# Attention's values made once per token and copied to their windows, 4 KB runs in the last stage, and column factors in PSUM in the sampling stage

## What is computed

```python
x = x + deformable_conv(group_norm(x))     # 8 groups, 9 points each, bilinear sampling, mask
t = tokens(x)
t = t + local_attention_block(layer_norm(t))   # 8 heads of 32, values of 16
t = t + moe_ffn(layer_norm(t))             # 8 experts, the best 2 for each token, 128 -> 512 -> 128
# inside the attention block: each token looks at itself and 32 tokens on either side
scores[w] = q[s] . k[s + w - 32] / sqrt(32) + rel_bias[w]     # w = 0..64, NEG outside the image
out = softmax(scores) @ v[s - 32 .. s + 32]
# moe: out[token] = weight[0] * expert_a(token) + weight[1] * expert_b(token)
```

## Time and profile before

| | us |
|---|---|
| three timed runs | 1660.62, 1667.56, 1667.63 (median 1667.56) |
| profiled execution, own time | 1650.45 |
| its span, first to last instruction | 1648.6 |
| PE busy | 1273.7 (77%) |
| DVE busy | 1039.2 (63%) |
| ACT busy | 762.2 (46%) |
| POOL busy | 631.1 (38%) |
| mean granted TensorE clock | 0.89 of full speed |

### The profile page before, as it was taken

How to read it: one execution, slowest core, us unless ns; L and a number is a source line. 1 busy time by engine, 2 the same in 40 slices (tenths; PEclk the granted TensorE clock), 3 DMA queues, 4 the chain that set the end, 5 groups by cost and what they waited for, 6 DMA issues and landing times. The chain is left out here.

```text
span 1648.6 us, 42938 instructions
## 1 busy us (share of the span) xinstructions
PE 1273.7 (77%) x13859; PEld 827.0 (50%) x13860; DVE 1039.2 (63%) x2372; ACT 762.2 (46%) x2018; POOL 631.1 (38%) x678
## 2 busy tenths in 40 slices
PE   4962898888989875898787888577752389999974
PEld 1541343433434322666565666233322389999972
DVE  4995889889898422676576677256553434444435
ACT  1212443444434260655454555375551157777650
POOL 2000788877878600000000000005677445555550
PEclk9995899999999995999899999797765589999995
DMA  3000000000000000000000000401111122222219
GB/s 112 0 0 11 0 1 1 0 0 0 0 0 0 5 0 25 3 4 4 4 4 4 3 4 4 164 1 37 43 48 50 47 54 66 68 68 68 66 53 304
DMA packets 56950, 54.72 MB, mean 33 GB/s; under 512 B 10335, under 2 KB 48735, under 8 KB 56439
## 3 DMA queue, kind: packets, MB, share of 16 engines
q1 hardware_dynamic: 46071, 31.12, 6.7%
q0 software_dynamic: 8448, 17.58, 3.2%
q10 hardware_dynamic: 2304, 4.20, 0.7%
HBM read 29.93 MB, written 23.00 MB: 32 GB/s over the span
## 5 line engine op out<-in xcount | busy, mean ns | idle before, releaser
L2073 ACT ACTIVATE e_hT<-e_ph,e_b 128x128 f32<-128x128 f32 x544 | 155.4, 369 | 74.7 <-PE e_ph L2030 58.1
L433 POOL TENSOR_TENSOR s_pc<-s_wide,VP 128x512 f32<-128x512 f32 x112 | 157.1, 1403 | 53.8 <-ACT s_wide L506 47.1
L1326 ACT ACTIVATE a_E<-a_E,a_nm 128x96 f32<-128x96 f32 x512 | 142.7, 361 | 68.7 <-DVE a_nm L1402 68.4
L424 POOL TENSOR_TENSOR s_acc<-s_acc,s_pb 128x512 f32<-128x512 f32 x112 | 153.9, 1374 | 40.6 <-DVE s_pb L585 39.0
L656 PE MATMUL s_pbc<-s_AT,s_sel 120*128 120x512 bf16 x400 | 135.3, 388 | 40.0 <-DVE s_pa L585 26.9
L1596 POOL MEMSET m_total<- 128x8 f32 x1 | 0.1, 110 | 410.7 <-POOLq L1138 410.7
L667 PE MATMUL s_pout<-s_pa,s_opT 128*128 128x512 f32 x288 | 151.6, 607 | 0.0
L2041 PE MATMUL e_py<-e_w,e_hT 128*128 x1088 | 149.3, 280 | 1.8 <-ACT e_hT L2073 1.2
L2030 PE MATMUL e_ph<-e_xT,e_w1s 128*128 128x128 f32 x1088 | 147.2, 279 | 1.0 <-issue 0.7
L1612 POOL DMA_INDIRECT slots<-m_pay,m_pos x128 | 127.7, 998 | 42.2 <-issue 42.2
L2011 POOL DMA_INDIRECT picks<-e_yw,e_rows x136 | 134.7, 991 | 22.5 <-POOL e_tick L2009 20.6
(11 more groups left out here) (218 smaller groups left out, 2518.1 us busy)
## 6 DMA issues: line engine op xcount, KB each, us to landing
e_rows<-slots SPq DMA_DIRECT2D x136, 66.0 KB
c_y<-picks SPq DMA_DIRECT2D x32, 256.0 KB
X<-in_x SPq DMA_DIRECT2D x8, 512.0 KB, 8.3
e_w<-in_w SPq DMA_DIRECT2D x2, 2048.0 KB, 12.7
out<-c_o ACTq DMA_DIRECT2D x16, 256.0 KB
picks<-e_yw,e_rows POOLq DMA_INDIRECT x136
slots<-m_pay,m_pos POOLq DMA_INDIRECT x128
m_pad<-in_c_pad SPq DMA_DIRECT2D x1, 1056.0 KB, 4.9
```

What stands on the lines that cost most here:

```text
L424: nc.gpsimd.tensor_tensor(acc[j][:], before, prod_b[b % 3][:], ALU.add)\
L433: nc.gpsimd.tensor_tensor(prod_c[k][:].rearrange("p (a b) -> p a b", a=HALF), wide[k][:].rearrange("p (a b) -> p a b", a=HALF), window(n, ...
L1326: act.activation(E[u % 2][:, o, :], E[u % 2][:, o, :], ACT.Exp, bias=nm[:, u % 2, o:o + 1]).then_inc(powered, 1)
L2073: ins = act.activation(hT[j % 2][:, q, :], p_h[j % 2][:, q * P:(q + 1) * P], ACT.Gelu, bias=b1[:, bass.ds(e, 1), q:q + 1].rearrange("p o h ...
```

## The change

In **sampling**, `A` and `rest` are laid out with the window's row outermost, so that the split into parts is one instruction of 800 elements where there were four of 200. The column factors of one token tile at a time (216 elements) are copied by ACT into PSUM, behind `A` (`place`, new line 474), and `PR` is made in 4 steps of 648 elements, one for each token tile, that read `MY` from SBUF and the factors from PSUM (new line 556). The column factors have one place only: ACT copies the next tile's when DVE has used the last ones. `weights` has 14 steps, not 13.

In **attention**, `v` is made by token, once: 4 matmuls of 128 tokens for each half in one product, in unit 2, taken out into `VT`. The output projection of unit 2 now stands ahead of the values' matmuls, and unit 3 has no product. SP then copies `VT` to the windows `V` with 12 DMAs for each half (32 partitions, 4 blocks of 544 bytes on each), which PE waits for once per half (`windowed`), in unit 0.

In the **last stage**, `c_dest` puts the two results of a token side by side and the four tokens that one partition needs next to each other: 8 rows of 512 bytes in one run of 4 KB. SP loads a chunk with one DMA of 512 KB, DVE adds its halves into a buffer of its own, and SP waits for that addition instead of the transposes.

The diff, cut to its core:

```diff
@@ sample_fast
-        A = p_A[:, 0:TPC * GROUPS * WIN5].rearrange("p (t g w) -> p t g w", t=TPC, g=GROUPS)
+        NA_ = TPC * GROUPS * WIN5
+        A = p_A[:, 0:NA_].rearrange("p (a u b) -> p a u b", a=5, b=5)
+        A_rows = p_A[:, 0:NA_].rearrange("p (a t w) -> p a t w", a=5, t=TPC)
+        cols_ = p_A[:, NA_:NA_ + 3 * GK].rearrange("p (q k) -> p q k", q=3)
...
-        STEPS = 2
+        STEPS = 1 + TPC
...
+                def place(c, t):
+                    if t:
+                        act.wait_ge(step, c * STEPS + t + 1)
+                    else:
+                        act.wait_ge(sized, c * 2 + 2)
+                    act.activation(cols_, fac[:, 1, :, t], ACT.Copy).then_inc(placed, 1)
...
+                        if t in PLACES and (not known(c) or c + 2 < NCH):
+                            place(c + 2, PLACES.index(t))
...
-                    elif k < 4:
+                    elif k < STEPS:
                         if k == 1:
                             dve.wait_ge(step, b + 1)
-                        q = k - 1
-                        ins = dve.tensor_tensor(
-                            PR[:, q].rearrange("p r t k -> p r (t k)"), MY[:].rearrange("p r t k -> p r (t k)"),
-                            fac[:, 1, q].rearrange("p (o t) k -> p o (t k)", o=1).to_broadcast([P, 3, TPC * GK]),
-                            ALU.mult)
-                        if q == 2:
-                            ins.then_inc(step, 1)
+                        s = k - 1
+                        dve.wait_ge(placed, c * TPC + s + 1)
+                        dve.tensor_tensor(
+                            PR[:, :, :, s],
+                            MY[:, :, s].rearrange("p (o r) k -> p o r k", o=1).to_broadcast([P, 3, 3, GK]),
+                            cols_.rearrange("p q (o k) -> p q o k", o=1).to_broadcast([P, 3, 3, GK]),
+                            ALU.mult).then_inc(step, 1)
@@ attention
         def plan(s):
             return ([(0, "q", m, s + 1) for m in range(2)] * ahead + [(1, "k", m, s + 2) for m in range(2)] * keys
-                    + [(2, "v", m, s + 1) for m in range(2)] * ahead + [(2, "o", 0, s - 1)] * out
-                    + [(3, "v", m, s + 1) for m in range(2, 4)] * ahead)
+                    + [(2, "v", 0, s + 1)] * ahead + [(2, "o", 0, s - 1)] * out)
...
+                def windows(s):
+                    for g in range(TPC):
+                        for k in range(3):
+                            at = s % 2 * NB + g + 1 - k
+                            lo = 1 if s % 2 == 0 and (g, k) == (0, 2) else 0
+                            hi = TPC - 1 if s % 2 == 1 and (g, k) == (TPC - 1, 0) else TPC
+                            last = at + (hi - 1) * UB + 1
+                            sp.dma_start(
+                                V[k * QB:(k + 1) * QB, at + lo * UB:last:UB].rearrange("p b h w -> p b (h w)"),
+                                VT[s % 2][g * QB:(g + 1) * QB, lo:hi].rearrange("p b h w -> p b (h w)"))\
+                              .then_inc(windowed, 16)
+                for s in range(NS):
+                    sp.wait_ge(dve_took, values_at(s))
+                    if s >= 2:
+                        sp.wait_ge(mixed, (s - 1) * US)
+                    windows(s)
...
-                        for b in range(UB):
-                            at = (m * UB + b) * QB
-                            last = pe.matmul(out[0:QW, b * P:(b + 1) * P], XS[j][:, at:at + QW], wv[:],
+                        for b in range(TPC):
+                            last = pe.matmul(out[:, b * P:(b + 1) * P], XS[j][:, b * P:(b + 1) * P], wv[:],
...
-                            if u == 1:
-                                pe.wait_ge(dve_took, start(s)[1])
+                            if u == 0:
+                                pe.wait_ge(windowed, (s + 1) * (16 * COPIES))
@@ combine
-                        sp.wait_ge(turned, c - NB + 1)
-                    for k in range(2):
-                        src = picks[k * TOK + c * CH:k * TOK + (c + 1) * CH, :]
-                        sp.dma_start(y[k][j][:], src.rearrange("(t p) c -> p t c", p=P)).then_inc(y_in[j], 16)
+                        sp.wait_ge(both, c - NB + 1)
+                    src = picks[2 * c * CH:2 * (c + 1) * CH, :]
+                    sp.dma_start(y[j][:], src.rearrange("(p t k) c -> p t k c", t=TPC, k=2)).then_inc(y_in[j], 16)
...
-                        dve.tensor_tensor(y[0][j][:], y[0][j][:], y[1][j][:], ALU.add).then_inc(both, 1)
+                        dve.tensor_tensor(yy[j][:], y[j][:, :, 0], y[j][:, :, 1], ALU.add).then_inc(both, 1)
```

More of the change, by code:

```diff
@@ L550, in weights @@
                         else:
-                            dve.wait_ge(step, b + 2)
+                            dve.wait_ge(step, b + STEPS)
                             dve.wait_ge(cleared, c + 1)
@@ L1093, in start, with values_at @@
             return len(kinds), len(kinds) - kinds.count("q"), kinds.count("q")
+        def values_at(s):
+            items = LEAD if s == 0 else plan(s - 1)
+            base = 0 if s == 0 else start(s - 1)[1]
+            taken = [x[1] for x in items if x[1] != "q"]
+            return base + taken.index("v") + 1
         def numbered(s, unit=None):
@@ L1265, in _ @@
                     product(*x)
-                scores(0, 0, 0, (2, 8))
+                scores(0, 0, 0, (2, 5))
                 def body(s, place, n=None):
@@ L2129, in combine @@
     with ExitStack() as st:
-        y = [[sb(nc, st, f"c_y{c}{j}", [P, TPC, P]) for j in range(NB)] for c in range(2)]
+        y = [sb(nc, st, f"c_y{j}", [P, TPC, 2, P]) for j in range(NB)]
+        yy = [sb(nc, st, f"c_yy{j}", [P, TPC, P]) for j in range(NB)]
         o = [sb(nc, st, f"c_o{j}", [P, CH]) for j in range(NB)]
```

87 lines of the change are left out of this document (49 added, 38 removed).

## The result

| | before | the change |
|---|---|---|
| runs, median (lowest to highest) | 1664.09 (1658.96 to 1667.63) | 1619.03 (1613.1 to 1628.0) |
| ratio, 95% interval | | 0.974 (0.9695 to 0.9786) |
| profiled execution, span | 1648.6 | 1620.6 |

What follows compares the result with a forecast made beforehand. No single engine bounds the program: DVE steps beside PE in sampling, PE in attention, DMA in the last stage. 18.9 + 1 + 8.4 + 52.5 + 6 = 86.8 us off 1650.45 gives 1563.7, median 1580; range 1548 to 1616.

Steps and rivals of the forecast that it cites:

- 18.9: Sampling loop: cheaper products less one new wait save 1.35 us a chunk, in 14 chunks 18.9 us.
- nothing: Sampling: merged splits save DVE 0.2 us where PE is the bound, so they gain no time.
- The port theory: Sampling: DVE products with two SBUF operands and POOL's work hinder each other; with one operand in PSUM they do not.
- Attention's lead: Ahead of attention's loop: three value products of 2.81 us each go, saving 8.4 us.
- A half is 3.5 us shorter: Attention's loop: fewer products and shorter PE waits save 3.5 us a half, in 15 halves 52.5 us.
- a set has landed 7.3 us after the take: Attention: 12 copies at 0.46 us issue plus 2.2 landing fit in 10.0 us, 2.7 to spare, costing nothing.
- the rival of late copies: Attention: copies take 1.0 us of queue each, a set 14 us; some 55 us lost, 1636 us; chance 0.08.
- the forecast 326: Attention, first to last score: 378.5 us before less the forecast 52.5.
- The zero in the sum: Stages without changed instructions, the experts among them: forecast difference 0 us.
- 420 GB/s: Last stage: loads in 4 KB runs reach the input image's rate, a chunk 1.87 instead of 2.28 us, saving 6 us.
- 358 GB/s: Last stage: memory limit per core from the Trainium skill; a chunk could reach only 2.20 us, the term -1.2 us.
- the two losses together: Range's upper end, 1616 us: sampling gives nothing (chance 0.13) and attention is bound by its score-to-transpose chain (chance 0.13).

Runs made afterwards that it cites:

- Sampling alone: The kernel before with only the change's sampling part put in: 1595.38 against 1620.51 us, ratio 0.9851.
- attention alone: The kernel before with only the change's attention part put in: 1589.07 us, ratio 0.982.
- b_before: The kernel before, unchanged, as a kernel of its own for a second profile, on a chip of the faster kind: 1622.90 against 1620.58 us, ratio 1.0016.
- r_after2: The change itself, unchanged, run again on the same chip as b_before: 1564.24 us, ratio 0.9665 to the kernel before.
- thin copies: The change with each of attention's 12 copies a half moving one partition's 544 bytes only, values wrong: 1553.04 against 1620.51 us.

## Why the prediction was wrong

**Sampling: right, mis-sized low.** 18.9 was 14 times 1.35. The first two chunks and the steps ahead of them gave 7.4 us (first residual 208.4 to 201.0; 207.4 to 202.8 in the pair on the faster chip), and the 12 distances behind them 1.70 each (25.58 to 23.88 in the mean), 27.9 in all. The products gave 3.46 against 4.95, so 1.49 a chunk. The other 0.21 is what the kernel with SBUF factors kept, whose products are no faster than before: it belongs to the rest of this part, in which the merged splits, called "nothing", are the likeliest source (they save DVE 0.6 us a chunk; no run took them alone). The port theory is shown by the run with SBUF factors. The Trainium skill, page "SBUF — State Buffer", section "SBUF: two separate sides", says that a DVE instruction with two SBUF inputs and a POOL one exclude each other for a whole instruction; 1294 ns against 818 agrees with a loss on DVE's side.

**Attention's lead: right.** From the first product to the first score 28.8 us became 20.4 (627.86 to 656.62, 601.75 to 622.16), 8.4 as forecast. Two microseconds were lost ahead of it, from sampling's last residual to the first product (60.3 to 62.1). Sampling alone has them too (62.1), attention alone has not (60.1); why is open.

**Attention's halves: wrong, and here is the failed step.** "A half is 3.5 us shorter" subtracted PE's work and PE's waits for DVE, each at its duration, and took it that what was left would keep its pace, with the copies costing nothing. It kept it only in part. On the chip of `b_before` 29.0 us came of 52.5. PE's groups of scores and values there, before and then the change:

```profile
L1225 PE MATMUL a_ps<-a_KT,a_Q 32*32 32x96 f32 x4096 | 65.3, 258 | 16.6 <-issue 13.8 <-DVE a_E L1396 1.2 <-DVE a_KT L1377 0.9
```
```profile
L1274 PE MATMUL a_ps<-a_KT,a_Q 32*32 32x96 f32 x4096 | 67.2, 260 | 31.0 <-issue 27.7 <-DVE a_E L1450 1.6 <-DVE a_KT L1428 0.9
L1301 PE MATMUL a_po<-a_V,a_PT 96*32 96x17 f32 x3904 | 47.5, 187 | 10.9 <-DMA a_V<-a_VT 7.2 <-issue 2.8
```

From the first to the last score, PE's time of 377.2 and 348.2 us is made up so:

| us | b_before | r_after2 | difference | forecast |
|---|---|---|---|---|
| PE busy | 320.8 | 288.0 | -32.8 | -45 |
| idle, "issue" | 13.8 | 32.2 | +18.4 | 0 |
| idle, for the copies | 0 | 7.2 | +7.2 | 0 |
| idle, for DVE and ACT | 42.6 | 20.8 | -21.8 | -7.5 |
| sum | 377.2 | 348.2 | -29.0 | -52.5 |

- The waits for DVE shrank by more than was forecast. What ate the gain is pauses put down to issue, busy time, and late copies.
- The copies cost 8 to 15 us, by the run without their bytes. Their step, "a set has landed 7.3 us after the take", took the issue at 0.46 us; it was 0.60 with pauses, 10.7 for a set against 9.7 available. This was the rival of late copies, at a fifth of its price, and nine copies remove its wait.
- PE's busy time fell by less, though the value products took 48.9 us less: the rest of PE's work took longer, the transposes 75.4 us where they had taken 70.3. The granted clock stood at its lower level (0.50) for 40 us of this stretch, 28 before.
- The pauses put down to issue are, by their timing, waits for instructions. The traces have the start and length of each 16 KB packet. In the kernels' 18 profiles 265 such pauses of PE in attention are longer than 0.6 us, and 262 of them end 1.15 to 1.9 us after a packet has ended; of its 242 pauses of that length with another cause 53 do, about what chance gives at one packet in 4.8 us. In `r_after2`, for instance, a packet started at 848.07 us and took about 1 us, and PE's pause of 3.67 us ended at 850.73. `b_before` has 5 such pauses, `r_after2` 19 and the kernel without the copies' bytes 19 (32.6 us of "issue" in all against 16.4 in the first profile of before). Packets come no more often in the change. Why they are late there is argued: each unit runs 64 scores and 64 values products with their weight loads, and the long products between them left time to bring the next. No run changed the supply alone.
- Not all of this idle time is lost time. The kernel with nine copies and the projection in unit 3 has as much of it (35.6 us) and yet comes to 330 to 334 us, within 8 of the forecast 326.

With thin copies the loop's three passes gained 32.6 us (298.1 to 265.5) and the straight code ahead of it and behind it 5.6 (80.3 to 74.7), 38.2 in all.

The Trainium skill, page "Runtime: NRT & Kernel Launch", section "Instruction fetch mechanics", has engines refilled in 16 KiB blocks through a DMA queue of their own, with the cost of a block's boundary mostly hidden and a stall at a branch. The 16 KB packets and the gaps at the loop's jump (3.5 to 5.2 us) agree; "mostly hidden" does not hold for PE here, with 32 to 37 us of issue gaps in the kernels without the long products.

Before, a gap of this kind stood in the profile too, at each of the loop's two jumps back; the earlier trace rows were taken from a half that had none. Over the loop's second pass a half took 101.9/4 = 25.5 us, over all three 298.1/12 = 24.8, not 23.4. A forecast from the clean half could not see that part of this time was of another kind.

**Untouched stages: taken as fixed.** On three chips they were, within 3 us. On the first chip they took 25 us more in the change's profile than in before's, and the two parts of this differ. The 15.5 us of norms and dispatch: the gaps of ACT, DVE and PE fall while POOL's scattering DMAs run, and in that profile their place moved from the end of the stage to its middle. The change's code does not do this each time: with the factors in SBUF, on a chip of the slower kind too, the gap stood at the end and the stage took 276.8. What moves it stays open. The 9.5 us of the experts go with the kernel, though no instruction of that stage was changed: 280.5 before, but 289.4 to 291.1 in three kernels with attention's change and twelve copies on chips of the slower kind, and 285 with nine copies. On the faster chips it is 279, 281.3 to 281.8, and 278. The zero in the sum was wrong there; the cause is open.

**The last stage: half the forecast.** It took 42.6 to 44.4 us in five profiles without this part and 39.0 to 42.4 in eleven with it, 3.2 less in the mean. 420 GB/s were taken from loads that wait for no buffer; three buffers gave 349 over 30 us, with 306 to 392 in windows of 10, and four 381 over 28 us. The step that failed is that the rate of the input load carries over to a stage that waits for its buffers. The 358 GB/s that the Trainium skill names (page "DMA: Bandwidth & Descriptors", section "Specifications") and that the prediction weighed was no limit either.

**Range.** Its upper end was meant as the two losses together. With the rivals' own prices (1583.6 and 18 us more in the profile) that is 1618, not 1616; the measured 1619 lies above both.

The sum of the terms on the faster chip, -60, lies within the forecast's range as a ratio (0.9665, the range reached 0.969), with the mechanism in attention wrong all the same; on the first chip it does not.

## What to carry to other kernels

Take a stage's length over a whole pass of its loop, gaps at jumps included, and expect idle time that waits for nothing visible to grow when long instructions are removed from between short ones; the times of the instruction packets tell whether it is a wait for them. When a copy takes the place of computing, count its issue on the queue by the nearest shape (here 0.6 us for 32 partitions and 128 runs), and see which of the copies can be saved by reading in place: three of twelve were free to drop, which took away the wait for them (8 us in the profile) and 12.5 us of the total. Before a stage is declared bound by memory, give it one more buffer.

## What the runs showed of the hardware

- A DVE product with both operands in SBUF took 1294 ns beside POOL's work, 818 ns with one of them in PSUM, 832 ns from SBUF with POOL idle.
- Removing long matmuls between runs of small ones doubled PE's gaps put down to issue (14 and 16 us to 32 and 37 in all). Of the 265 over 0.6 us, 262 ended 1.15 to 1.9 us after a 16 KB instruction packet had ended. After one of the longer ones the clock was at its lower level (granted 0.50 from 837 to 840).
- The same program differs by up to 44 us between chips (medians of 1620 to 1621 against 1654 and 1664). In two profiles of it 33 us apart (1615.6 and 1648.6), 29 lie in the stage where POOL scatters (248 and 277 us), where on the slower one ACT stood still for 30 us at a time.
- The experts' first layer (`e_ph`), unchanged, took 267.6 to 271.6 us on chips of the faster kind, by kernel and not by chip, and 270.3 to 280.1 on the slower kind; the cause is open.
